# Two heads per projection matmul, and half of the keys doubled by a transfer

## The reference

```python
q = jnp.einsum('bxy,iyk->bxik', x, Wq).reshape(h, b, t, hs)
k = jnp.einsum('bxy,iyk->bxik', x, Wk).reshape(h, b, t, hs)
v = jnp.einsum('bxy,iyk->bxik', x, Wv).reshape(h, b, t, hs)
wei = jnp.einsum('hbqd,hbkd->hbqk', q, k) * hs ** (-0.5)
wei = jnp.where(causal, wei, -jnp.inf)
out = jnp.einsum('hbqk,hbkd->hbqd', jax.nn.softmax(wei, axis=-1), v)
```

## Time and profile before

| | us |
|---|---|
| median of 3 runs | 2094.62 (2094.47 to 2095.85) |
| profiled execution, its own time | 2098.11 |
| its span, first to last instruction | 2096.4 |

### The profile page before, as it was taken

The page is one execution under the profiler, slowest core; times in us unless marked ns, Lnnn a source line. Parts: engine busy times, 40 slices in busy tenths (PEclk is TensorE's granted clock), DMA queues, the critical chain, the costliest instruction groups (busy, mean ns, idle before and its releaser), DMA issues. The chain is left out here.

```text
span 2096.4 us, 63859 instructions
## 1 busy us (share of the span) xinstructions
PE 1705.4 (81%) x21906; PEld 1485.2 (71%) x21907; DVE 1256.0 (60%) x2999; ACT 1066.6 (51%) x3094; POOL 783.9 (37%) x1054
## 2 busy tenths in 40 slices
PE   2898888888888888898888898734899999999930
PEld 1787777778778777787787787624678777787820
DVE  4577777667667676776676777558333333333337
ACT  4565766666666666666666656410233333333324
POOL 1133444335334443453353443310344444444411
PEclk9999999999999999999999999855899999999965
DMA  5322221322232223223222211036111111111136
GB/s 140 122 97 87 86 69 62 105 77 67 67 102 76 69 84 97 67 64 97 87 67 64 89 49 36 6 136 259 31 34 35 36 33 33 36 33 35 35 113 210
DMA packets 139465, 162.02 MB, mean 77 GB/s; under 512 B 78334, under 2 KB 110206, under 8 KB 136832
## 3 DMA queue, kind: packets, MB, share of 16 engines
q1 hardware_dynamic: 128128, 136.94, 20.2%
q0 software_dynamic: 6912, 17.84, 2.7%
q10 hardware_dynamic: 4224, 4.19, 0.6%
HBM read 93.92 MB, written 66.06 MB: 76 GB/s over the span
## 5 line engine op out<-in xcount | busy, mean ns | idle before, releaser
L1354 ACT ACTIVATE act_g<-ps_e,b 128x128 f32<-128x128 f32 x576 | 164.7, 369 | 352.3 <-PE ps_e L1317 328.6
L1317 PE MATMUL ps_e<-xt,wres 128*128 128x128 f16 x3456 | 295.6, 225 | 3.5 <-issue 3.3
L1317 PEld LDWEIGHTS ps_e<-xt,wres 128*128 x3456 | 240.3, 97 | 54.9 <-issue 7.3
L1375 DVE SCALAR_TENSOR_TENSOR e_y<-ps_e,b 128x256 f32<-128x256 f32 x72 | 30.6, 425 | 333.2 <-PE ps_e L1328 333.2
L876 POOL TENSOR_TENSOR o_st<-o_norm,o_st 128x256 f16<-128x256 f32 x128 | 86.0, 672 | 380.9 <-ACT o_st L589 380.9
L1288 POOL DMA_INDIRECT z_scr<-e_y,rows_out x72 | 130.1, 1807 | 245.4 <-DVE e_y L1375 239.8
L577 ACT ACTIVATE probs<-ps,nbias 128x128 f32<-128x128 f32 (+1 forms) x512 | 211.0, 417 | 8.4
L1328 PE MATMUL ps_e<-wres,g_hi 128*128 x1152 | 195.9, 275 | 9.9 <-issue 4.2
L381 PE MATMUL ps<-x_hi,w_q 128*128 128x128 f16 x2048 | 197.0, 222 | 2.6 <-issue 2.3
L381 PE MATMUL ps<-x_hi,w_k 128*128 128x128 f16 x2048 | 187.2, 219 | 0.2
L381 PE MATMUL ps<-x_lo,w_q 128*128 128x128 f16 x1024 | 182.3, 222 | 0.0
(11 more groups left out here) (259 smaller groups left out, 4803.9 us busy)
## 6 DMA issues: line engine op xcount, KB each, us to landing
piece<-in_moe_w SPq DMA_DIRECT2D x24, 768.0 KB, 6.4
w_scr<-piece_pair SPq DMA_DIRECT2D x24, 768.0 KB, 4.4
wres<-w_scr SPq DMA_DIRECT2D x18, 1024.0 KB, 22.1
v_scr<-v_tok SPq DMA_DIRECT2D x32, 512.0 KB, 2.6
v_pos<-v_scr SPq DMA_DIRECT2D x32, 512.0 KB, 4.3
z_scr<-zero SPq DMA_DIRECT2D x32, 256.0 KB, 3.7
f_z<-z_scr SPq DMA_DIRECT2D x8, 1024.0 KB, 5.6
x_t<-in_xT SPq DMA_DIRECT2D x32, 128.0 KB, 6.0
```

The source lines that it names most:

```text
L1317: last = mm(out, w[:, b, c * FF + f * P:c * FF + (f + 1) * P], xt[:, p, a, c], start=(m == 0), stop=(m == 5))
L1354: nc.scalar.activation(act_g[:, p, f], ps[:, 3 + 2 * p + f // 4, (f % 4) * P:(f % 4 + 1) * P], ACT.Gelu, bias=bias[:, f:f + 1], scale=1.0 ...
```

## The change

- A query or key matmul takes two different heads, h and h + 8, in place of one head twice: `wqk` holds for each of 8 pairs the columns of both. Query and key have two fills each instead of four, six in all with the two of the values, in groups 7 (two), 0, 2, 4 and 5.
- A fill has head 4n + i on partitions 0 to 63 and head 8 + 4n + i on 64 to 127. It is evicted by two ACT and two DVE instructions of 64 x 512. ACT writes both halves to partitions 0 to 63 (`q_st` or `k_pair[.., 0, ..]`). DVE writes the low part, for the query to partitions 64 to 127 of `q_st`, for the key to partitions 0 to 63 (`k_pair[.., 1, ..]`).
- The keys have to stand on both halves of the partitions, so SP copies `k_pair` of a tile (8 KB on each of 64 partitions) from 0 to 63 to 64 to 127 with one transfer, after the last fill's low part. PE waits for it (`s_kdup`) ahead of the scores of group 0. In SP's order it stands behind the results of tile s - 2 and ahead of the piece of weights.
- `q_hi`, `lo_rows` and its two POOL instructions go; DVE's query form becomes the key's. ACT no longer waits for a free `q_hi`.
- `s_fill_hi` and `s_fill_lo` now count evictions (`NOPS` = 10 per tile) and not fills.

```diff
-FILLS = [("v", 0), ("q", 0), ("v", 1), ("q", 1), ("q", 2), ("q", 3), ("k", 0), ("k", 1), ("k", 2), ("k", 3)]
+FILLS = [("v", 0), ("q", 0), ("v", 1), ("q", 1), ("k", 0), ("k", 1)]
...
-FILLS_OF_SLOT = [[2, 3], [], [4], [5], [6, 7], [8], [9], []]
+PAIRS = H // 2
+
+
+OPS_BEFORE = [sum(1 if kind == "v" else 2 for kind, _ in FILLS[:j]) for j in range(NF + 1)]
+NOPS = OPS_BEFORE[NF]
+V_OPS = OPS_BEFORE[3]
+FILLS_OF_SLOT = [[2], [], [3], [], [4], [5], [], []]
...
-    wqk = {n: sb("w2_" + n, [P, 2, KC, H, 2, HS], F16) for n in "qk"}
+    wqk = {n: sb("w2_" + n, [P, 2, KC, PAIRS, 2, HS], F16) for n in "qk"}
...
+            if "A" in stages:
+                t = s + 1
+                sp.wait_ge(s_fill_lo, NOPS * (t + 1))
+                sp.sem_inc(s_held_sp, 1)
+                sp.dma_start(k_pair[HS:P, q], k_pair[0:HS, q]).then_inc(s_kdup, 16)
...
             if since(t, 1) or j >= 2:
-                pe.wait_ge(s_fill_lo, NF * t + j - 1)
+                pe.wait_ge(s_fill_lo, NOPS * t + (OPS_BEFORE[j - 1] if j else OPS_BEFORE[NF - 1] - NOPS))
...
-                        last = mm(bank[:, hh * P:(hh + 1) * P], w[:, b, c, h].rearrange("p k d -> p (k d)"), xs[a][:, c],
+                        last = mm(bank[:, i * P:(i + 1) * P], w[:, b, c, 4 * n + i].rearrange("p k d -> p (k d)"), xs[a][:, c],
...
             if g == 0:
-                pe.wait_ge(s_fill_lo, NF * (t + 1))
+                pe.wait_ge(s_fill_lo, NOPS * (t + 1))
+                pe.wait_ge(s_kdup, 16 * (t + 1))
...
+            to = q_st[:, p] if kind == "q" else k_pair[:, p, 0]
+            for a in range(2):
+                src = ps_a[j % 2][a * HS:(a + 1) * HS].rearrange("p (h t) -> p t h", h=4)
+                nc.scalar.activation(to[0:HS, :, PAIRS * a + 4 * n:PAIRS * a + 4 * n + 4], src, ACT.Copy).then_inc(s_fill_hi, 1)
...
+            high = (q_st[:, p] if kind == "q" else k_pair[:, p, 0])[0:HS]
+            low = q_st[HS:P, p] if kind == "q" else k_pair[0:HS, p, 1]
+            for a in range(2):
+                dve.wait_ge(s_fill_hi, NOPS * t + OPS_BEFORE[j] + a + 1)
+                at = slice(PAIRS * a + 4 * n, PAIRS * a + 4 * n + 4)
+                src = ps_a[j % 2][a * HS:(a + 1) * HS].rearrange("p (h t) -> p t h", h=4)
+                stt(out=low[:, :, at], in0=src, scalar=1.0, in1=high[:, :, at], op0=ALU.mult, op1=ALU.subtract).then_inc(s_fill_lo, 1)
```

More of the change, by code:

```diff
@@ L86, in attention_block @@
     causal = sb("causal", [P, P], F16)
-    lo_rows = sb("lo_rows", [P, 1], F32)
     head_rows = sb("head_rows", [P, HB, CTX], F16)
@@ L123, in attention_block @@
         for n in "qk":
-            for copy in range(2):
-                pairs.append((ld[n], 16, stage[n][:].rearrange("p c (h d) -> p c h d", d=HS),
-                              [wqk[n][:, k, :, :, copy, :] for k in range(2)], WA_UP))
+            for a in range(2):
+                pairs.append((ld[n], 16, stage[n][:, :, a * PAIRS * HS:(a + 1) * PAIRS * HS].rearrange("p c (h d) -> p c h d", d=HS),
+                              [wqk[n][:, k, :, :, a, :] for k in range(2)], WA_UP))
         pairs.append((ld["v"], 16, stage["v"][:], [wv[:, k] for k in range(2)], WA_UP))
@@ L164, in _ @@
                                     pattern=[[-1, P]], channel_multiplier=1).then_inc(s_const, 1)
-            nc.gpsimd.affine_select(out=lo_rows[:], in_=lo_rows[:], compare_op=ALU.is_gt, fill=-1.0, base=HS,
-                                    pattern=[[0, 1]], channel_multiplier=-1).then_inc(s_const, 1)
             nc.gpsimd.affine_select(out=head_rows[:], in_=head_rows[:], compare_op=ALU.is_ge, fill=0.0, base=0,
                                     pattern=[[-DK, HB], [0, CTX]], channel_multiplier=1).then_inc(s_const, 1)
-            pool.wait_ge(s_const, n + 6)
+            pool.wait_ge(s_const, n + 5)
             nc.gpsimd.affine_select(out=head_rows[:], in_=head_rows[:], compare_op=ALU.is_ge, fill=0.0, base=DK - 1,
@@ L251, in attention_block @@
     s_z_out = sem("s1_z_out")
+    s_kdup = sem("s1_kdup")
     s_xb, s_mv1, s_mv2 = sem("s1_xb"), sem("s1_mv1"), sem("s1_mv2")
@@ L303, in step @@
                 t = s + 1
-                sp.wait_ge(s_fill_hi, NF * t + V_FILLS)
+                sp.wait_ge(s_fill_hi, NOPS * t + V_OPS)
                 sp.sem_inc(s_held_sp, 1)
-                sp.wait_ge(s_fill_lo, NF * t + V_FILLS)
+                sp.wait_ge(s_fill_lo, NOPS * t + V_OPS)
                 sp.sem_inc(s_held_sp, 1)
@@ L375, in fill @@
             else:
-                for hh in range(4):
-                    h = 4 * n + hh
+                for i in range(4):
                     w = wqk[kind]
@@ L386, in scores @@
             if g == 0:
-                pe.wait_ge(s_fill_lo, NF * (t + 1))
+                pe.wait_ge(s_fill_lo, NOPS * (t + 1))
+                pe.wait_ge(s_kdup, 16 * (t + 1))
             if since(t, 1) or g:
                 pe.wait_ge(s_exp, 2 * (GROUPS * t + g))
-            qs, kh, kl = (m[:, p, g * GTOK:(g + 1) * GTOK].rearrange("p t h -> p (t h)") for m in (q_st, k_hi, k_lo))
+            qs, kh, kl = (m[:, g * GTOK:(g + 1) * GTOK].rearrange("p t h -> p (t h)")
+                          for m in (q_st[:, p], k_pair[:, p, 0], k_pair[:, p, 1]))
             mm(ps_s[:, 0:P], qs[:, 0:P], kh[:, 0:P], start=True, stop=False, skip_group_check=True)
@@ L558, in hi @@
             if kind == "v":
-                src = ps_a[j % 2].rearrange("p (h d) -> p h d", d=HS)
-                dst = v_tok[:, p, 8 * n:8 * n + 8, 0]
-            elif kind == "q":
-                if since(t, 1) or j >= 3:
-                    act.wait_ge(s_fill_lo, NF * t + j - 1)
-                src = ps_a[j % 2].rearrange("p (h t) -> p t h", h=4)
-                dst = q_hi[:, j % 2]
-            else:
-                src = ps_a[j % 2].rearrange("p (h t) -> p t h", h=4)
-                dst = k_hi[:, p, :, 4 * n:4 * n + 4]
-            nc.scalar.activation(dst, src, ACT.Copy).then_inc(s_fill_hi, 1)
+                nc.scalar.activation(v_tok[:, p, 8 * n:8 * n + 8, 0], ps_a[j % 2].rearrange("p (h d) -> p h d", d=HS),
+                                     ACT.Copy).then_inc(s_fill_hi, 1)
+                return
+            to = q_st[:, p] if kind == "q" else k_pair[:, p, 0]
+            for a in range(2):
+                src = ps_a[j % 2][a * HS:(a + 1) * HS].rearrange("p (h t) -> p t h", h=4)
+                nc.scalar.activation(to[0:HS, :, PAIRS * a + 4 * n:PAIRS * a + 4 * n + 4], src, ACT.Copy).then_inc(s_fill_hi, 1)
         def exps(t, g):
@@ L677, in lo @@
                     op0=ALU.mult, op1=ALU.subtract).then_inc(s_fill_lo, 1)
-            elif kind == "q":
-                src = ps_a[j % 2].rearrange("p (h t) -> p t h", h=4)
-                stt(out=q_st[:, p, :, 4 * n:4 * n + 4], in0=q_hi[:, j % 2], scalar=lo_rows[:, 0:1],
-                    in1=src, op0=ALU.mult, op1=ALU.add).then_inc(s_fill_lo, 1)
-            else:
-                src = ps_a[j % 2].rearrange("p (h t) -> p t h", h=4)
-                at = (slice(None), p, slice(None), slice(4 * n, 4 * n + 4))
-                stt(out=k_lo[at], in0=src, scalar=1.0, in1=k_hi[at],
-                    op0=ALU.mult, op1=ALU.subtract).then_inc(s_fill_lo, 1)
+                return
+            high = (q_st[:, p] if kind == "q" else k_pair[:, p, 0])[0:HS]
+            low = q_st[HS:P, p] if kind == "q" else k_pair[0:HS, p, 1]
+            for a in range(2):
+                dve.wait_ge(s_fill_hi, NOPS * t + OPS_BEFORE[j] + a + 1)
+                at = slice(PAIRS * a + 4 * n, PAIRS * a + 4 * n + 4)
+                src = ps_a[j % 2][a * HS:(a + 1) * HS].rearrange("p (h t) -> p t h", h=4)
+                stt(out=low[:, :, at], in0=src, scalar=1.0, in1=high[:, :, at], op0=ALU.mult, op1=ALU.subtract).then_inc(s_fill_lo, 1)
         def maxima(t, g):
```

9 lines of the change are left out of this document (3 added, 6 removed).

## The result

The changed kernel takes 2123.5 us (median of 4, 2121.5 to 2124.5) against 2094.6 us of the kernel before (2094.3 to 2095.9, on the same chip): 1.0136 times as long, 95% interval 1.0118 to 1.0153. It is slower by 29 us, clear of the noise but under 2%, where 58.5 us less were forecast. The profiled execution has a span of 2121.6 us.

A forecast was written before the change was run, and what follows sets the result against it. The prediction took a loop of waits between DVE, ACT and PE as the bound, not PE alone. Twelve iterations gaining 1.12 + 3.10 us (50.6) plus 7.8 outside gave 58.5 off 2094.6: 2036 us, range 1995 to 2078.

The forecast's parts named there:

- The bound, read from the page and the timelines: Attention steps: a loop of waits between DVE, ACT and PE sets the pace, not PE alone despite 81% busy.
- Rival (a): Attention phase: PE does bound, all 172 us come, 1923 us; half of it gives 2009; chance 0.07.
- Groups 0 and 6, PE's clock: Removed fills: 1.9 us earlier in group 6, 1.22 gained in group 0, with matmul durations kept.
- rival (b): Group 0: PE's idle of about 2 us lowers the clock, 1.7 us in 19 steps, 32 us, 2068; chance 0.11.
- The price of a half: Query and key evictions: 64 partitions cost what a whole one does, 0.48 us on ACT, 0.61 on DVE.
- The step without a loop turn: Ordinary attention step of 40.18 us: the group-by-group walk gains 1.12 us.
- The step with a turn: Step of 42.28 us: gains 3.10 us, keeping the 3.35 us stall at the loop's head and 3.6 us slow clock.
- The transfer: Key copy ahead of the next tile's group 0 scores: takes 2.6 to 4.3 us of 5.6 available, hidden.
- The first tile: Nothing hides the transfer: 5.4 us of fills saved against about 4 to 5 us added, nothing taken.
- Steps outside the loop: Seven filling steps outside the loop gain 1.12 us each, 7.8 us together.

The follow-up runs named there:

- e11: Changed kernel without the third term of cross-attention times values, two idle f32 matmuls each in groups 6 and 0, 20 one-column matmuls once ahead of the loop: 2055.9 us.
- e13: Changed kernel without the third term of cross-attention times values, 40 idle one-column matmuls once ahead of the loop: 2122.8 us.
- e12: e7 without the third cross-attention term, two idle f32 matmuls each in groups 6 and 0, 20 one-column matmuls once ahead of the loop: 1985.6 us.
- e14: Changed kernel with 30 idle one-column matmuls (60 instructions) once ahead of the loop, the loop itself untouched: 2151.9 us.
- e8: Changed kernel without the third term of cross-attention times values, with two idle f32 matmuls each in groups 6 and 0 of every step: 2145.3 us.
- e10: e7 without the third term of cross-attention times values, with two idle f32 matmuls each in groups 6 and 0: 2072.5 us.
- e16: e15 with 118 idle one-column matmuls (236 instructions) once at the very start: 1994.2 us.
- e2: Changed kernel with each half of an eviction written to the partitions it is read from, on ACT and DVE: 2127.4 us.
- e3: Changed kernel with one whole ACT and one whole DVE eviction per query or key fill, second half of the heads left out: 2015.9 us.
- e4: Changed kernel without the transfer that doubles the keys and without PE's wait for it, upper half of the keys zero: 2117.8 us.
- e7: Changed kernel with whole evictions of query and key fills and twelve transfers a step placing the heads' rows, everything computed: 2019.7 us.
- e15: e7 with one idle f32 matmul in group 6 and one in group 0, inside the loop only, everything computed: 2050.9 us.
- e9: Changed kernel without the third term of cross-attention times values, nothing added: 2144.2 us.
- e5: Changed kernel with two idle f32 matmuls of 512 columns each in groups 6 and 0 of every step: 2130.1 us.
- e1: Changed kernel with eight idle f16 matmuls of 512 columns each in groups 6 and 0: 2130.1 us.
- e6: Changed kernel with eight idle one-column matmuls each in groups 6 and 0 of every step: 2166.9 us.

## Why the prediction was wrong

*The bound, read from the page and the timelines*: right as far as it goes. Rival (a), PE binds, would have given iterations near 72 us and all 172 us; even with the clock up an iteration took 78.53 (e11).

*Groups 0 and 6, PE's clock*: **this is the step that failed**, and what came is rival (b), which had a chance of 0.11 and half of the price. The walk moved PE's waits about and kept its durations, so the clock stands in the sum at nothing. It had foreseen 2 us of idle in group 0 (measured: 1.86) and priced what follows at 1.7 us in 19 steps, 32 us, in the rival alone. Of group 6 it said that PE's minus is worth little since L474 waits for DVE anyway, and asked no further. But L474 followed the key fill without a gap; without that fill (1.34), and with a pair of halves where one whole eviction stood ahead of DVE's low part L775, which ends the wait, 2.24 are idle. (The 1.61 of the earlier trace rows is another place, ahead of L482 in group 7; it shrank to 0.29.) Behind the wait of group 6 the transposes and the value fill, behind group 0 the transposes and the scores run at the lower clock, and they are on the path: with the third place of group 3, 66.9 us in all 31 steps (e13 to e11). The argument against (b), that 1.6 of idle had left the clock at 1.00 in the earlier trace rows, was no safe bound: in group 3 of the changed kernel 1.50 and 0.84 leave it there in one step and not in another.

The section of the Trainium skill named beside (b) ("TensorE: Matmul & The Clock Gate", "HAM oscillation — how this bites in real kernels") describes a PE that waits between bursts and restarts at half clock. The trace shows this: 0.57 and 0.60 behind 2.24 and 1.86 of idle. The waits in the section's own example are longer, so what waits of 2 us do is told by these rows. With (b) as the forecast the number would have been 2068, still 55 too low.

*The price of a half*: too low. "Costs what a whole one does" held for the duration (689 beside 692 ns), not for the pitch: 1.20 and 1.40 for a pair where 0.48 and 0.61 from start to start gave 1.08 and 1.30 (0.48 + 0.60, 0.61 + 0.69). That is 0.1 for a pair on each engine. A bigger thing lay beside it: the prediction called the removed and the added evictions even in number and placed them, but never asked what whole evictions would be worth. They are worth 70 us (e12 to e11), more than the whole forecast gain.

*The step without a loop turn*: forecast 39.06, measured 39.83 with the clock up (e11) and 42.10 without. So the group-by-group walk was good to 0.8 us where its durations held.

*The step with a turn*: "I keep both" (the stall and the slow stretch behind it) failed. The stall vanished, as the loop's new length and place happened to suit. The forecast 39.18 *included* the stall; e11 took 38.70 without one. In e14 the stall is worth 28.4 us in 11 turns, 2.6 each (for 4.7 of idle a turn; the kernel before has 3.2), so the walk of this step was up to 2.1 too low, and the vanished stall hid it. That is luck: with the stall kept, as forecast, the changed kernel took 2151.9 (e14). What takes its place in that step was not traced.

*The transfer*: hidden, as forecast; 4.1 us to landing. The estimate of 4.4 from the Trainium skill ("SBUF — State Buffer", "Door 1: The DMA port swizzle" and the section behind it) was the better one against 2.6, and neither end mattered. *The first tile*, "nothing taken", cost: the copy of its output (`o_t`) starts at 99.44 in place of 96.15, and leaving the transfer out gives 5.8 us.

*Steps outside the loop*, forecast to gain 1.12 each: from the first `o_t` to the fourth 117.0 us pass before (96.15 to 213.12) and 116.9 in e11 (99.36 to 216.27); from the 28th to the last it is 152.3 in both. Nothing gained, 7.8 missing; why is open.

Together: 2123.5 - 2036 = 87.5, of which the clock is 66.9, the first tile about 3.3, the steps outside 7.8, the iteration (78.53 for 78.24, twelve times) 3.5. Some 6 us are left unassigned. These are e11's and e13's figures, which leave out one term of the cross-attention; that cut alone is worth 0.7 us (e13 to the changed kernel). The chances put 0.87 on faster on the strength of a walk in which one rival, the likeliest, was priced from a single row of the clock.

## What to carry to other kernels

When a change takes work from an engine that is not the bound, its idle places grow, and for TensorE that has a price: look in the timeline for each idle place that will grow, ask what filled it before, and price what stands behind it on the path also at the slow stretch's pace (here 1.7 times as long). A wait that left the clock up once is no proof that it always will (1.50 did both here). Idle matmuls in the place are a quick test. Split evictions cost per instruction and not per partition (689 ns for 64 partitions, 692 for 128), so look for a layout in which they stay whole and let transfers do the placing while the queues are idle. When two kernels differ at all in instruction count, compare the packets of the instruction queue and the "issue" idle at the head of the loop before reading anything else into the difference.

## What the hardware showed that I hadn't expected

*The stall at the head of PE's loop depends on the loop's place in the program.* Without it the instruction queue moves 43 to 45 packets, with it 142 to 144 (172 in the kernel before, whose loop has 2,140 instructions), some 9 per turn, and PE idles 2.6 to 6.4 us at the head of every turn (in e8 and e10 at two places of it). Moving a loop of 1,749 instructions by 60 brought it (e14, +28.4 us); moving one of 1,685 by 80 removed it (e13, -21.4 us); moving one of 1,770 by 236 removed it (e16, -56.6 us). All kernels here agree with one rule, which is inferred and not shown: seven blocks of 256 instructions stay at hand (a packet is 0.72 MB / 44 = 16.4 KB), and a loop that touches an eighth is fetched again at every turn. The counts behind it, from the built programs:

| kernels | loop starts after | its length | stall |
|---|---|---|---|
| changed, e2, e3 | 3,305 | 1,749 | no |
| e4; e7 | 3,304; 3,309 | 1,748; 1,752 | no |
| e13; e11; e12 | 3,305; 3,305; 3,309 | 1,685; 1,719; 1,722 | no |
| e16 | 3,545 | 1,770 | no |
| e15 | 3,309 | 1,770 | yes |
| e9; e8; e10 | 3,225; 3,265; 3,269 | 1,685; 1,719; 1,722 | yes |
| e5; e14; e1 and e6 | 3,345; 3,365; 3,385 | 1,783; 1,749; 1,815 | yes |

Where the blocks begin is free. Of blocks of 64, 128, 256 or 512 and any number of them, only seven of 256 sort all the kernels rightly, the kernel before among them. By it a loop of up to 1,792 instructions can be placed well, the less easily the longer it is, and the kernel before can't be.

*The clock's price is paid behind the wait, and by other matmuls than those that waited.* 2.24 us of idle turned 0.53 into 0.88 for three transposes and 0.59 into 1.06 for two matmuls of 512 columns, and four f32 passes of 592 ns in each of the two gaps gave it back (granted clock 0.91 to 0.99), although PE then does more work: its busy time from 400 to 1300 us goes from 727.56 (changed kernel) to 778.84 (e11) while the kernel gets 3% faster. They also cleared the third place, where they don't stand.
